# Sending rows with long ties to a late batch, and a rolled-up repeat round, in a top-p attention kernel

## What is computed

```python
def _top_p_attention(X, W1, W2, W3):
    q = X @ W1.T @ W2.T
    k = X @ W3.T
    logits = q @ k.T / TAU
    probs = jax.nn.softmax(logits, axis=-1)
    idx = jnp.argsort(-probs, axis=-1)
    sp = jnp.take_along_axis(probs, idx, axis=-1)
    cs = jnp.cumsum(sp, axis=-1)
    keep_sorted = cs - sp < TOP_P
    ...
    A = probs * mask
    return A / jnp.maximum(A.sum(-1, keepdims=True), 1e-12)
...
for n in range(STEPS):
    A = _top_p_attention(Xa, W1, W2, W3)
    Xf = R @ Xf
    Xa = A @ Xa
    Z = Z + Xf @ U1[n].T + Xa @ U2[n].T
```

## Time and profile before

| | us |
|---|---|
| three runs | 2754.72, 2742.20, 2745.24 |
| median | 2745.24 |
| profiled execution, its time | 2751.88 |
| its span, first to last instruction | 2750.1 |
| TensorE busy in it | 2367.2 |
| VectorE busy in it | 2200.9 |
| ScalarE busy in it | 1070.2 |
| GpSimd busy in it | 138.5 |
| mean granted TensorE clock | 0.933 |

### The profile page before, as it was taken

The page is one execution under the profiler, slowest core; times in us unless marked ns, Lnnn a source line. Parts: engine busy times, 40 slices in busy tenths (PEclk is TensorE's granted clock), DMA queues, the critical chain, the costliest instruction groups (busy, mean ns, idle before and its releaser), DMA issues. The chain is left out here.

```text
span 2750.1 us, 53658 instructions
## 1 busy us (share of the span) xinstructions
PE 2367.2 (86%) x17795; PEld 1996.2 (73%) x17795; DVE 2200.9 (80%) x6636; ACT 1070.2 (39%) x1803; POOL 138.5 (5%) x342
## 2 busy tenths in 40 slices
PE   7999999868889887888887649987999999999985
PEld 2666666556667776767775549985999999999952
DVE  3777777588887888888889677766999999999836
ACT  4666666533323333333332130003434434434323
POOL 0000000101111111000010010000000000000000
PEclk8999999989899998999988869998999999999997
DMA  3000000022122221222221135542333343434220
GB/s 130 2 1 2 1 1 1 2 100 79 73 76 101 92 88 54 97 98 101 101 101 50 52 153 201 201 171 104 127 127 126 116 137 105 146 103 138 91 89 25
DMA packets 57330, 245.05 MB, mean 89 GB/s; under 512 B 6929, under 2 KB 18576, under 8 KB 43344
## 3 DMA queue, kind: packets, MB, share of 16 engines
q1 hardware_dynamic: 57040, 241.99, 25.2%
HBM read 235.15 MB, written 6.82 MB: 88 GB/s over the span
## 5 line engine op out<-in xcount | busy, mean ns | idle before, releaser
L2058 PE MATMUL a_acc<-H,pT 128*128 128x128 f32 x4056 | 548.0, 277 | 10.4 <-ACT a_rows L2090 3.8
L2058 PEld LDWEIGHTS a_acc<-H,pT 128*128 128x128 f32 x4056 | 495.5, 192 | 27.5 <-DVE pT L2192 18.7
L976 PE MATMUL small<-XR,wT 128*128 128x128 f32 x2756 | 373.3, 280 | 29.9 <-ACT wT L1230 29.3
L976 PEld LDWEIGHTS small<-XR,wT 128*128 128x128 f32 x2756 | 339.1, 195 | 45.8 <-ACT wT L1230 45.8
L850 PE MATMUL lg<-kT,qs 128*128 128x512 f32 (+1 forms) x742 | 341.0, 596 | 30.6 <-ACT e L1152 20.4
L71 DVE MAX8 cand<-e 128x8 f32<-128x64 f32 (+3 forms) x1898 | 302.8, 240 | 56.9 <-issue 34.1
L2192 DVE TENSOR_TENSOR pT<-a_tr,a_adjT 128x512 f32<-128x512 f32 (+1 forms) x546 | 316.6, 645 | 22.4 <-PE a_tr L2017 19.2
L880 PE MATMUL accR<-XR,adj 128*128 128x129 f32 x2704 | 327.9, 283 | 0.0
L880 PEld LDWEIGHTS accR<-XR,adj 128*128 128x128 f32 x2704 | 324.7, 200 | 0.0
L2017 PE MATMUL a_tr<-ident,prob 128*128 128x128 f32 x2028 | 312.4, 274 | 10.9 <-ACTq L2084 10.9
L1230 ACT ACTIVATE wT<-tr 128x512 f32<-128x512 f32 (+1 forms) x371 | 206.1, 566 | 246.7 <-PE tr L966 245.7
(11 more groups left out here) (344 smaller groups left out, 2485.1 us busy)
## 6 DMA issues: line engine op xcount, KB each, us to landing
adj<-in_adjT SPq DMA_DIRECT2D x52, 1664.0 KB, 7.2
g_adj<-in_adjT SPq DMA_DIRECT2D x26, 1664.0 KB, 6.8
a_adj<-in_adj SPq DMA_DIRECT2D x26, 1664.0 KB, 6.8
a_adjT<-in_adjT SPq DMA_DIRECT2D x156, 256.0 KB, 3.9
a_adjT<-in_adjT SPq DMA_DIRECT2D x26, 128.0 KB, 4.1
XT<-in_x_t SPq DMA_DIRECT2D x1, 1664.0 KB, 7.1
hT_scratch<-hT SPq DMA_DIRECT2D x1, 1664.0 KB, 12.0
nsT_scratch<-nsT SPq DMA_DIRECT2D x1, 1664.0 KB, 5.3
```

What stands on the lines that cost most here:

```text
L976: mm = eng.matmul(accA[:, :], wT[(k * NC + c - 1) % 2][:, o:o + P], xa[:, j, 0:P], start=(j == 0), stop=(j == T - 1))
L2058: mm = eng.matmul(acc[:, :], pT[g % RING][:, (j % 4) * P:(j % 4 + 1) * P], H[:, j, :], start=(j == 0), stop=(j == T - 1))
```

## The change

Three things are changed; all of them stand in VectorE's stream.

1. In `Search.end` for the pairs of step 1, backward rows count as open ones while a scalar `late` is 0: they get a slot in the batch. When `late` is 1 they are handled in the pair, as before. `assign_slots(p)` sets `late` for pair p+1: 1 where the number of slots taken up to pair p, over all partitions, is above 80. The counts are worked out a few instructions later in `end`, from the new value.
2. `select` gets a register `late`; the drop pass of a pair runs only where it is above 0. The batch keeps its drop pass.
3. `another_round`'s 10 halvings become a loop, and the block of three rounds ahead of the nested loops is gone, so that the round stands once in each `select`.

```diff
+ROOM_FOR_TIES = 80
...
+        eng.memset(self.one("late", 0), 0.0)
...
+            if spills:
+                late, base, opened = self.one("late", 0), self.counts[:, 1, 0:1], self.counts[:, 0, 0:2]
+                eng.tensor_tensor(all_of("sharp"), all_of("partial"), all_of("backward"), ALU.subtract)
+                eng.scalar_tensor_tensor(all_of("gone"), all_of("backward"), late, all_of("backward"),
+                                         ALU.is_gt, ALU.mult)
+                eng.tensor_scalar(all_of("backward"), all_of("backward"), late, None, ALU.mult)
+                eng.drain()
+                eng.tensor_tensor(opened, opened, all_of("gone"), ALU.max)
...
         eng.drain()
+        if spills:
+            eng.tensor_tensor(self.counts[:, 1, 1:2], base, opened[:, 0:1], ALU.add)
...
-        step = FIRST_STEP
-        for n in range(ROUND_HALVINGS):
+        with eng.Fori(0, ROUND_HALVINGS):
...
-                with eng.Fori(0, 3):
-                    with eng.If(eng.snap(flag) > OPEN - 1):
-                        another()
                 while_over(eng, flag, OPEN - 1, self.width // 8, another)
...
-            if both_ways:
+            if late is not None:
+                with eng.If(eng.snap(late) > 0):
+                    self.drop_ties(eng, k)
+                    eng.drain()
+            elif both_ways:
                 self.drop_ties(eng, k)
...
+                        eng.tensor_copy(find.flag_int[:, 2:3], find.one("late", 0)[0:1, :])
...
+                        eng.reg_load(late, find.flag_int[0:1, 2:3])
...
+                        eng.tensor_scalar(find.one("late", 0), slots[:, 3:4], float(ROOM_FOR_TIES), None, ALU.is_gt)
```

More of the change, by code:

```diff
@@ L95 @@
              "r_above0", "r_theta", "r_below", "r_was", "r_stays", "r_moves", "r_tau", "r_hi", "r_value", "r_bound",
-             "r_above", "r_known", "r_up", "r_mass")
+             "r_above", "r_known", "r_up", "r_mass", "r_step", "r_half", "r_low", "gone", "late", "sharp")
     def __init__(self, sb, width):
@@ L290, in end @@
         eng.tensor_scalar(all_of("backward"), all_of("partial"), 0.5, None, ALU.is_lt)
-        if spills:
-            base, opened = self.counts[:, 1, 0:1], self.counts[:, 0, 0:2]
-            eng.tensor_tensor(self.counts[:, 1, 1:2], base, opened[:, 0:1], ALU.add)
-            for n in (2, 3):
-                eng.scalar_tensor_tensor(self.counts[:, 1, n:n + 1], opened[:, 0:1], base, opened[:, 1:2],
-                                         ALU.add, ALU.add)
         eng.drain()
@@ L312, in end @@
         eng.drain()
+        if spills:
+            eng.tensor_tensor(self.counts[:, 1, 1:2], base, opened[:, 0:1], ALU.add)
+            for n in (2, 3):
+                eng.scalar_tensor_tensor(self.counts[:, 1, n:n + 1], opened[:, 0:1], base, opened[:, 1:2],
+                                         ALU.add, ALU.add)
         if not both_ways:
             eng.tensor_copy(all_of("strict"), all_of("partial"))
-        eng.tensor_tensor(all_of("levels"), all_of("levels"), all_of(strict), ALU.mult)
+        eng.tensor_tensor(all_of("levels"), all_of("levels"), all_of("sharp" if spills else strict), ALU.mult)
         eng.tensor_scalar(all_of("scale"), all_of(strict), 2.0 ** -24, 1.0 - 2.0 ** -24, ALU.mult, ALU.add)
@@ L451, in keep, with select @@
                                  accum_out=self.one("kept", k))
-    def select(self, eng, k, e_pad, kind, flag, regs, both_ways, found=False):
+    def select(self, eng, k, e_pad, kind, flag, regs, both_ways, found=False, late=None):
         def another():
@@ L1390, in _ @@
                 regs = [eng.alloc_register(f"group_flag{q}") for q in range(4)]
+                late = eng.alloc_register("late_flag")
                 eng.memset(kT[half_of[1], :], 0.0)
@@ L1437, in assign_slots @@
                         eng.drain()
-                        eng.scalar_tensor_tensor(find.flag_int[:, :], find.both("over_full")[0:1, :], float(OPEN),
+                        eng.tensor_copy(find.flag_int[:, 2:3], find.one("late", 0)[0:1, :])
+                        eng.scalar_tensor_tensor(find.flag_int[:, 0:2], find.both("over_full")[0:1, :], float(OPEN),
                                                  find.flag_top[:, :], ALU.mult, ALU.add)
@@ L1464, in select @@
                         find.select(eng, k, e[b][k][:, :], kinds[k], flag, regs, step == 1,
-                                    found=step == 1 and not at(p, PAIRS))
+                                    found=step == 1 and not at(p, PAIRS),
+                                    late=late if step == 1 and not at(p, PAIRS) else None)
                         if step == 1:
```

27 lines of the change are left out of this document (15 added, 12 removed).

## The result

| | us |
|---|---|
| before, median of 4 runs | 2743.72 (2739.11 to 2754.72) |
| changed kernel, median of 4 runs | 2721.64 (2720.50 to 2722.70) |
| ratio, 95% interval | 0.9915, 0.9896 to 0.9933 |
| changed kernel, profiled execution | 2720.61, span 2718.8, mean granted clock 0.945 |
| TensorE, VectorE busy in it | 2347.7, 2156.6 |

The change saves 22 us, 0.85%. The forecast was 30 us; the direction holds and the time lies inside the range, above the forecast by 6.6 us.

What follows compares the result with a forecast made beforehand. TensorE was taken as the bound, with VectorE costing it waits in step 1. Six terms, five gains less a loss in the last pair, summed to 30.1 us off the 2745.24 median: 2715 us, range 2700 to 2734.

Steps and rivals of the forecast that it cites:

- Three signs: Expected flag waits near 0.25 up to pair 11, flags to adjacency 7.2 to 8.2 us, stalls well under 30 us.
- 1. pair 0: TensorE's 11.29 us wait for tile 0 shrinks as VectorE comes 3.8 earlier, less 0.6 added: 3.2 us.
- 2. flag waits, pairs 1 to 11: TensorE's six waits ahead of the flags, 17.6 us without the last one, all go down to 0.25 each: 16.1 us.
- 3. pair 6: Of TensorE's 11.0 us wait in pair 6 only 5.4 come back, since ScalarE is next to be late.
- 4. pair 8, tile 1: TensorE's wait there falls from 1.15 to 0.25 us: 0.9 us.
- 5. clock, flags to adjacency: Three longer flag waits go, so matmuls from flags to adjacency run at the higher clock: 6 us, bounds 0 and 6.
- 6. the last pair: Search uncovered by TensorE, drop passes still there; added instructions lose about 2 us, taken as 1.5 us lost.
- Added: Search stages, slot instructions and load, and select's branch cost VectorE 1.5 us a pair, hidden under TensorE in pairs 0 to 11.
- The shorter repeat round: Only the jump over it counts; stalls taken as gone in pair 8, worth about 3 us of the sum.
- VectorE as the bound throughout: Rival: VectorE bounds all of step 1, each of 14 passes pays in full, 53 us, time 2692; chance 0.08.
- The waits moved: Rival: ScalarE or adjacency loads replace the flag waits, leaving 12 us gain, time 2733; chance 0.15.
- The slower end: Rival: batch slots overflow, repeat rounds of some 35 us run uncovered in the last pair, 2755 to 2825; chance 0.05.

Runs made afterwards that it cites:

- drains_inside: Changed kernel with select's drain moved into the branch on late, ahead of the drop pass, and the one behind the pass removed: 2714.41 us, ratio 0.9886.
- late_from_start: Changed kernel with the threshold at −1 and late set to 1 from the start, so all 27 drop passes run: 2756.03 us, ratio 1.0038.
- short_round_only: Kernel before with only the repeat round rolled up and standing once; all 27 drop passes stay: 2730.58 us, ratio 0.9944.
- ties_only: Changed kernel with the unrolled repeat round put back, twice in each select; 13 drop passes: 2740.43 us, ratio 0.9976.

## Why the prediction was right and wrong

**The bound, the place and the count** were right: 13 passes, `late` at pair 7, the flag waits up to pair 8 down to 0.9 us or less, most of the gain ahead of pair 7, no repeat round. Pair 6 came out in part: 3.82 us wait for ScalarE as forecast, but 2.55 still for `select`. Three signs did not come: the waits of 4.79 and 5.71 ahead of the flags of pairs 9 and 12 (forecast near 0.25, and 2 to 3), the stretch from flags to adjacency in pair 9, 9.26 us, and the stalls ahead of `keep` and the drop pass, 28.2 us together where "well under 30" was said.

**The sum against the trace.** Between the two profiled executions, the start of the flags of pair 0 had already moved by 1.6 us. The shorter round stands in step 0 too, but VectorE's first candidate instruction, ahead of any `select`, had already moved by 1.4 (30.00 to 28.59), and the stalls ahead of the cut in step 0 stayed (12.5 us in 13, then 12.3 in 13). From the flags of pair 0 to the batch's flags (1545.22 before, 1518.04 after) the lead grew to 27.2, so step 1 gained 25.6 where the terms had 30.1. The remaining 4 us of the difference between the two executions lie behind the batch, where the change has no instruction:

| term | predicted | in the two traces |
|---|---|---|
| 1. pair 0 | 3.2 | 2.9 (11.29 to 8.37) |
| 2. flag waits, pairs 1 to 11 | 16.1 | 10.6 (17.5 to 6.9, waits that are none counted as 0.25) |
| 3. pair 6 | 5.4 | 4.6 (11.00 to 2.55 and 3.82) |
| 4. pair 8, tile 1 | 0.9 | 0.9 |
| 5. clock, flags to adjacency | 6.0 | 6.3 (71.4 to 65.1 over pairs 1 to 9) |
| 6. the last pair | −1.5 | −4.0 (lead 31.2 at the flags of pair 11, 27.2 at the batch's) |

The rows add up to 21.3; the missing 4.3 of the 25.6 stand in no term. Part of it is the clock in pair 6, whose first transposes took 1.97 us and now 1.09.

**Term 2 failed at one place**, the 4.79 ahead of the flags of pair 9. The step said that "VectorE's lead after seven light pairs meets the 4.77". There was hardly a lead. VectorE can't run ahead freely: in the light pairs it waited for rows that ScalarE copies, 12.6 us in four waits in the changed kernel's list. Its timeline at the start of the search of pair 8, at the end of that search, and at the start of the search of pair 9:

```profile
1096.12 0.06 DVE L1435 MEMSET gate<- 128x1 f32 x1
...
1120.46 0.16 DVE L334 TENSOR_TENSOR pair_flags<-pair_flags,scalars 128x2 f32<-128x2 f32 x1
...
1170.90 0.06 DVE L1435 MEMSET gate<- 128x1 f32 x1 [3.00 <-issue]
```

The flags of pair 8 were written at 1120.6 and TensorE read them at 1121.79: 1.2 us of lead. From one search to the next VectorE takes 74.8 us (1096.12 to 1170.90), with a second mark and a stall of 3.00; TensorE, its wait of 4.79 left out, takes 68.9 from flags to flags (1121.79 to 1195.46). Ahead of pair 6, still in the light stretch, the lead was 6.6 us (flags written at 988.5, read at 995.14); pair 7, heavy and with only 65.1 us of TensorE beside it, used it up. With 1.36 left in drains_inside, both the laid-bare branches and the heavy pair 7 had their share.

**"Added" was mis-sized most.** It had 1.5 us a pair, hidden under TensorE, and so 1.5 in all. late_from_start shows 25.5 us of time for all of it with every drop pass in place, and 13 with the drains moved. The search grew by 0.2 to 1.0, 0.6 in the mean of pairs 1 to 12 (I had 0.7) and the loads' stall from 0.77 to 1.10 (I had 0.5 for it with two instructions): near enough. The branch was taken as 0.15 from a row in which the jump had been worked out already. Behind a `drain` with nothing running, the gap ahead of the cut is 0.4 to 1.1 us in most tiles, for it and the next branch. drains_inside gives 8 us back by moving one `drain`. That is also term 6: from the flags of pair 11 to those of the batch it takes 170.05 us before, 174.02 in the changed kernel and 170.25 in drains_inside.

**"The shorter repeat round" was mis-sized too.** The prediction counted 3 us for it; alone it gives 15.5 of the 22. I had seen 16 stalls and 30.9 us in the earlier trace rows, and still credited the waits that hang on them to the removed passes. Taking out 3.8 us of pass and taking out 1 to 3 us of stall are two ways to free the same waits, and the trace of before can't say which does it. What went wrong is that I priced the stalls in one pair only. That part should have been a term with bounds: 30.9 us of stalls in 16 tiles, none to all of them gone. The rule of the Trainium skill weighed there ("Runtime: NRT & Kernel Launch", Instruction fetch mechanics) pointed at all of these stalls; I applied it to pair 8 alone.

The two errors worked against each other. Without the shorter round's 3 and the added 1.5 the forecast had the passes alone at 28.6 us, and they measured 34 (29 with the drains moved). The jump gave 12 us more than counted, and the added instructions took up to 24 more. Taken in the order before, short_round_only, late_from_start, the change, these steps add up to the whole by construction; the check from another side is ties_only, 6.6 us where 34 less 25.5 makes 8. So the price of the passes held within a fifth, and that the time still fell into the range is in part luck, since two wrong terms nearly cancelled.

**From the trace to the median.** On the profiled execution's scale the forecast was 2721.8, and the changed kernel's profiled execution took 2720.61. But the median of before is 8 us under its own profiled execution, and that of the changed kernel 1 us over. The terms were read in an execution that was longer than most, and their sum was then taken off the median. If part of those 8 us were waits of step 1 that the change removes, they count in the sum and not in the median. Only one execution of before has a trace here, so that is argued and not shown.

**The rivals.** VectorE as the bound throughout is out: it had 53 us for the 14 passes, and they gave 34 with everything else equal. The waits moved only in pair 6, where it was forecast. The slower end was right as a mechanism and its price too low, 61 us a round. Its sums were off as well: two rounds of 35 on top of 2715 make 2785, not 2755, and four 2855, not 2825.

**Open.** Which tiles stall at a jump of given length: the stalls lie unevenly over the pairs, and no kernel moved the code without changing its length. The 11.6 us in three stalls ahead of a search (`gate`, line 1435), among them the 3.00 above, were there in every kernel (9.3 to 14.9 us in three); I tried nothing on them. Pair 6 light by itself was not tried.

## What to carry to other kernels

A pass that is taken away is worth its own time less what it covered: look at what the engine works out behind it (branches, register loads, drains) and at the brackets of the instruction after it. Where code that never runs is jumped over and the trace shows stalls at the landing, shorten that code first and by itself, for it can be worth more than the work you meant to save. And where a budget makes only some steps cheap, place them where the engine enters late or has least cover: with 13 drop passes in both, their place alone made 0.3%, and with 11 in both 0.16%, which lies within the intervals.

## What was not expected of the hardware

- The two branches in a light tile leave a gap of 0.67 and 1.06 us ahead of the cut when they stand behind a `drain` (601.68, 610.63), and 0.07 when that `drain` is gone and they are worked out under a 3.6 us pass (607.83).
- Stalls behind a jump fell as the code passed over got shorter, and VectorE's stream with it: 30.9 us in 16, 22.7 in 12, 7.5 in 4, for about 200, 100 and 80 listed rows.
- A third register load adds 0.33 us to a stall of 0.77 for two, and moving the loads behind other instructions moves the stall with them (14.3 us in 13 becomes 10.6 in 13) and leaves the time as it was.
- Behind one repeat round, where four register loads and the ends of the nested loops stand, VectorE did nothing for 16.5 us.
